# One step of an NF4 weight tile cut into two halves between the steps of the main work

## The reference, cut to what matters

```python
    def _dequant(codes, scales):
        w = NF4[codes]
        O, I = w.shape
        w = w.reshape(O, I // BLOCK, BLOCK) * scales[:, :, None]
        return w.reshape(O, I)
    def _lin_lora(x, W, A, B):
        base = jnp.einsum('bsh,oh->bso', x, W)
        lora = jnp.einsum('bsr,or->bso', jnp.einsum('bsh,rh->bsr', x, A), B)
        return base + lora
    q, k, v = (_lin_lora(x, _dequant(codes_attn[i], scales_attn[i]), ...) for i in range(3))
    attn = (q + k + v) / 3.0
    o = _lin_lora(attn, _dequant(codes_attn[3], scales_attn[3]), ...)
    x1 = x + o
    g = _lin_lora(x1, ...)          # 1792 features, gate
    u = _lin_lora(x1, ...)          # 1792 features, up
    h = jax.nn.silu(g) * u
    d = _lin_lora(h, ...)
    return x1 + d
x = x + _L0_attn_ref(_layernorm(x), ...)
x = x + _L0_ffn_ref(_layernorm(x), ...)
x = x + _L1_attn_ref(_layernorm(x), ...)
x = x + _L1_ffn_ref(_layernorm(x), ...)
```

## Time and profile before

| | |
|---|---|
| median of 3 runs | 804.11 us (802.1 to 804.88) |
| the profiled execution, its own time | 802.01 us |
| its span from first to last instruction | 800.7 us |
| TensorE busy | 718.0 us, 90% of the span |
| VectorE busy | 554.1 us, 69% |
| ScalarE busy | 448.2 us, 56% |
| GpSimd busy | 218.6 us, 27% |
| mean granted TensorE clock | 0.949 of 2.4 GHz |

### The profile page before, as it was taken

One profiled execution on the slowest core, in us unless ns is written; L12 is line 12 of the kernel. 1 busy time (PEld: TensorE's weight loads), 2 busy tenths in 40 slices (PEclk: granted clock), 3 DMA queues, 4 the chain that ended last, 5 costly groups with the idle time before them and its releaser, 6 DMA issues.

```text
span 800.7 us, 10753 instructions
## 1 busy us (share of the span) xinstructions
PE 718.0 (90%) x3832; PEld 535.9 (67%) x3832; DVE 554.1 (69%) x1065; ACT 448.2 (56%) x579; POOL 218.6 (27%) x208
## 2 busy tenths in 40 slices
PE   2898866999999998989988999988899999989998
PEld 1665422656677665667666777766677789967886
DVE  6979977563597767869798876667554434577883
ACT  3778787565877767877875722354432221244452
POOL 1023000004374653646577454211401000000000
PEclk9999966999999999989998999999999999979999
DMA  9636689867476677657765310201301011200001
GB/s 349 184 137 213 188 271 280 263 203 228 129 227 194 204 229 231 205 189 241 228 211 189 97 41 27 76 19 48 105 15 50 23 40 29 61 1 14 27 27 40
DMA packets 55541, 110.79 MB, mean 138 GB/s; under 512 B 9904, under 2 KB 20560, under 8 KB 55232
## 3 DMA queue, kind: packets, MB, share of 16 engines
q1 hardware_dynamic: 42912, 80.28, 31.4%
q10 hardware_dynamic: 8192, 15.73, 5.9%
q0 software_dynamic: 4384, 14.09, 5.9%
HBM read 92.19 MB, written 17.89 MB: 137 GB/s over the span
## 4 chain that ended last, share of the span: by engine, by line
PE 56%; DVE 19%; ACT 9%; issue 9%; DMA 4%; POOL 1%; ACTq 1%; SPq 1%; DVEq 0%; POOLq 0%
PE bank L1245 15%; PE bank L1247 14%; PE bank L1246 14%; ACT hot L1667 2%; PE bank L1359 2%; DVE x L2034 2%; DMA wide_buf<-in_down_flat 2%; ACT c L1627 2%; DVE bank L1949 2%; PE bank L1557 1%; DVE hot L1923 1%; PE bank L1372 1%; PE bank L1401 1%; DVE stats L1844 1%; ACT w_h L1675 1%
## 5 line engine op out<-in xcount | busy, mean ns | idle before, releaser
L1667 ACT ACTIVATE hot<-rep,levels 128x2048 f16<-128x2048 f16 x94 | 192.9, 2093 | 16.7 <-ACT c L1627 10.6
L1245 PE MATMUL bank<-zt_h,w_h 128*128 128x512 f32 (+1 forms) x232 | 94.8, 409 | 2.2 <-DVE zt_l L2022 2.0
L1247 PE MATMUL bank<-zt_h,w_l 128*128 128x512 f32 (+1 forms) x232 | 92.6, 399 | 0.0
L1246 PE MATMUL bank<-zt_l,w_h 128*128 128x512 f32 (+1 forms) x232 | 92.4, 398 | 0.0
L1245 PE MATMUL bank<-w_h,xq_h 128*128 128x512 f32 (+1 forms) x192 | 73.8, 384 | 2.2 <-ACT xq_l L1759 1.9
L1246 PE MATMUL bank<-w_l,xq_h 128*128 128x512 f32 (+1 forms) x192 | 71.6, 373 | 0.0
L1247 PE MATMUL bank<-w_h,xq_l 128*128 128x512 f32 (+1 forms) x192 | 71.5, 372 | 0.0
L1359 PE MATMUL bank<-hot,diag 128*32 128x512 f16 x856 | 64.7, 421 | 2.5 <-ACT hot L1667 2.5
L2178 POOL TENSOR_TENSOR q_a<-q_a,q_m 128x384 f32<-128x384 f32 (+3 forms) x34 | 35.7, 1051 | 85.1 <-DVE q_m L1808 85.0
L2240 POOL TENSOR_TENSOR at_l<-ztok,at_h 128x512 fp32r<-128x512 f32 x28 | 37.5, 1341 | 56.0 <-ACT at_h L1699 55.9
L1245 PEld LDWEIGHTS bank<-zt_h,w_h 128*128 128x128 f32 (+1 forms) x232 | 44.6, 192 | 12.0 <-DVE zt_l L2022 2.4
(11 more groups left out here) (221 smaller groups left out, 1703.1 us busy)
## 6 DMA issues: line engine op xcount, KB each, us to landing
rep<-codes SPq DMA_DIRECT2D x56, 512.0 KB, 4.7
codes<-c SPq DMA_DIRECT2D x28, 256.0 KB, 5.1
raw<-in_codes_gu_t ACTq DMA_DIRECT2D x14, 512.0 KB, 6.1
sc<-in_scales_gu_t SPq DMA_DIRECT2D x56, 128.0 KB, 3.2
raw<-in_codes_attn_t ACTq DMA_DIRECT2D x7, 512.0 KB, 3.8
raw<-in_codes_down_t ACTq DMA_DIRECT2D x7, 512.0 KB, 7.1
sc<-in_scales_down_t SPq DMA_DIRECT2D x28, 128.0 KB, 3.5
wide_buf<-in_gate_flat SPq DMA_DIRECT2D x5, 512.0 KB, 4.7
```

The lines of the kernel that those rows point to most:

```text
L1245: PE.matmul(psum, lh, rh, start=first, stop=False, **kw)
L1246: PE.matmul(psum, lh, rl, start=False, stop=False, **kw)
L1247: return PE.matmul(psum, ll, rh, start=False, stop=last, **kw)
L1667: S.activation(hots[plan.slot[hot_ring(t), (t, m)]][:], codes_in_place(t), ACT.Relu, bias=levels[:, at:at + 1], scale=levels[:, at + 1:at ...
```

## The change

The generator now yields twice per tile. The first half of step t holds the lookup of tile t, the LoRA product of tile t - 1, the parts of tile t - 2, the planes of tile t + 1. The second half holds the scaling of tile t itself and the transfer of scales. Rates are doubled, so that the same number of tiles goes by per main step. The two opening steps of the generator (its first loads; the planes of tile 0) aren't halved, so the tiles stand up to one step earlier in `stages`. `maxima` advances at half its rate while `until` runs before `attention`.

```diff
-EARLY_RATE = 0.7
-ATT_RATE = 0.5
-NF4_RATE = 0.43
+EARLY_RATE = 1.4
+ATT_RATE = 1.0
+NF4_RATE = 0.86
...
         if jobs[t // 2]["last"]:
             p.add("lora", t)
             p.note("made", t)
+            unsettled.append(t)
 
     def assemble(t):
...
-        if j["last"]:
-            unsettled.append(t)
...
             if t < tiles:
                 look(t)
             if t:
-                assemble(t - 1)
                 lora(t - 1)
             low_parts()
             if t + 1 < tiles:
                 hits(t + 1)
-            if t:
-                scales(t + 2)
             if t and u == 0:
                 if i > 1:
                     stacks(i - 1)
                 made[0] = i
+            yield
+            if t < tiles:
+                assemble(t)
+                scales(t + 3)
             yield
...
-    side_max = Side(greatest, MAX_RATE)
+    side_max = Side(greatest, MAX_RATE / 2)
     weave(stages(), Side(itertools.chain(int4_weights(), greatest), INT4_RATE), Side(ready_nf4, EARLY_RATE))
     until(n_attn - 1, side_max)
+    side_max.rate = MAX_RATE
```

## The result

The changed kernel takes 790.75 us, the median of 4 runs (787.44 to 791.87); the kernel before took 803.23 beside it (4 runs). The ratio is 0.984, 95% interval 0.981 to 0.987: faster by some 12.5 us, 1.6%, where 21 were forecast. The profiled execution took 790.65 us, span 789.3.

A forecast was written before the change was run, and what follows sets the result against it. TensorE was taken to set the pace from 200 to 480 us, waiting for late scalings and losing clock; VectorE and ScalarE from 60 to 137. Terms summed to -21.1 us, from 804.1 to 783 us, range 774 to 799.

The forecast's parts named there:

- rival A: All terms come as summed: 783 us, own range 774 to 791, chance 0.57.
- Rival B: The waits go but the clock doesn't come back: 792 us, range 789 to 799, chance 0.26.
- Waits of L1372: LoRA product waiting for its bank's scaling, 200 to 480 us: 16.8 us of waits, 4 left, so -12.8 us.
- The clock in that stretch: 200 to 480 us: of 11.2 us lost to slow clock, put down to these waits, 7.7 come back.
- Next in line: With TensorE faster in the stretch, planes and additions come late more often: +4 us, bounds 0 and +10.
- The start: Cast of token tile 1's high part slips behind the first plane: +3 us, bounds 0 and +6.8.
- Layer norms: 60 to 137 us: most of 4.1 us of waits for the sum behind the scaling goes: -2 us.
- one tile earlier: 100 to 137 us: ScalarE's queue, which TensorE waits for, holds one plane less: -2 us, bounds 0 and -4.
- Attention: Scaling of tile 20 moves ahead of what delayed it: 1.9 us of wait and 1.7 of clock, -3.6 us.
- D: Rival, down steps: the scaling pushes the additions, each costing 2.4 us; slower, 812 us at 12 tiles, chance 0.09.

The follow-up runs named there:

- kernel 12: The changed kernel measured once more, with nothing changed and a trace of its own: 788.86 us, ratio 0.982 to the kernel before.
- Kernel 10: The kernel before, with TensorE's waits of over 1 us for the bank filled by repeats of a lookup's first matmuls: 802.89 us, ratio 0.998.
- kernel 5: The kernel before, with scaling and load of next scales at the end of a still whole step from tile 23 on: 799.18 us, ratio 0.993.

## Why the prediction was right in kind and too large

The time lies in the range and in rival A's own range; 783 was 6 to 8 us too low. The time alone would not tell A from B: 790.75 lies in B's range too and nearer to its 792. What tells them apart is the clock. Two traces of the changed kernel give the terms (kernel 12 in second place).

- **Waits of L1372**, forecast -12.8: -16.1 and -16.6. Nearly nothing of them is left, where I had kept 4.
- **The clock in that stretch**, forecast -7.7: busy time for the same matmuls -7.5 and -7.1. Rival B, that the clock doesn't come back, fell: 1.00 instead of 0.96. Kernel 10 ties the slow slices to these places. The slow stretch at 340 us, for which the prediction had no wait in its rows, has one too, of 2.35 us up to 341.50.
- **Next in line**, forecast +4: +9.6 and +8.0 (all other waits of TensorE in the stretch, 5.6 us before, are 15.2 and 13.6). This is the term that was mis-sized most. The largest part is +5.9 and +4.2 for ScalarE's planes, and its cause was in no step of mine: I counted the moved `scales` as moved, but not that SP would stand in it with the spread of the codes behind. Kernel 6, with only that load put back, has 4.2 us of these waits instead of 8.4.
- **The start**, forecast +3, bounds 0 to +6.8: the first addition slipped by 5.5 us, the cast exactly as rows 9 had it, 18.84 to 25.63. By the last addition of the first product +3.9 and +3.0 were left, so this term was about right. The sign given for it was not: around 60 us the main work was up to 6.6 us behind, not 3 at most.
- **Layer norms** and **one tile earlier**, forecast -2 each: from the last addition of the first product to the merge it took 77.8 us before, 77.7 and 77.8 after, so 0 for both. These two terms are the step that failed. The waits for the sum behind the scaling did go, 4.1 to 0.3, and ScalarE's queue did hold one plane less. The third layer norm, from the last addition of the second product to the merge, became 4.1 and 3.8 us shorter. But the tile's work that left it now stands ahead of it, in the second product, where VectorE was already busy 32.2 of 34.6 us, and that stretch became 4.0 and 3.7 us longer. I had put this price at nothing. All eight traces with half steps have both (38.1 to 39.8 us and 39.0 to 41.2), all six with whole steps neither (34.1 to 34.7 and 42.6 to 44.7). That the moved tile is the cause is argued from the counts of instructions.
- **Attention**, forecast -3.6: 0 in the first trace, -4.8 in the second. The wait for the LoRA product went in both. What I had not seen is that the clock of this stretch is different from trace to trace, 0.90 and 0.97 here, by as much as the term: TensorE's busy time there is 53.9 us before, 54.3 and 50.8 after, its waits are 5.7, 5.3 and 4.0.
- **D**, the scaling pushes the additions: waits for x went from 1.7 to 4.2 and 3.5 us, where I had set "under 4", and far from the 10 of D. With whole steps (kernel 5) they are 9.6: additions do come late behind what stands ahead of them, and the halves hold it down.

By these terms the two traces give 3.8 + 0 - 14.1 = -10.3 and 3.0 - 4.8 - 15.8 = -17.6 up to the last `gu_mul`, and the spans fell by 11.4 and 17.6. The medians, 12.5 and 15.4 us below those beside them, lie between.

## What to carry to other kernels

A wait at one instruction is a matter of how far ahead its producer stands in the queues; but moving the producer without dividing the step handed most of the wait on to the work that then stood behind it (a gain of 4.8 us in the stretch, against 17.1 with the step divided). When a step is moved, follow its transfers too: a load that waits for the moved work holds every later transfer of the same issuing engine, and putting one load back was worth 6 to 9 us, about half of what the change itself brought. Work that is moved out of one stretch arrives in another: look at how busy the engines are there as well. Cut a stretch by marks of the work, not by fixed times: busy time and waits of the same matmuls then add up to its length, and the clock can be read apart from the waits. And take a second trace before a few microseconds in one stretch are explained.

## What the runs showed of the hardware

The granted clock over 10 us fell to about 0.84 beside waits of TensorE of 1.1 to 2.4 us, in the middle of dense work. With work put in at seven such places of the NF4 stretch (kernel 10) one slow slice was left of ten. In the NF4 stretches of all 14 traces the clock fell to the lower level 33 times, each time beside or shortly behind a wait of 1 us or more: for the scaling, for an addition to x, or for planes. The reverse doesn't hold: about half of such waits had no fall near them. The two traces of the changed kernel show it at the same lookup. In the first all slices from 200 to 520 us are at 1.00, in kernel 12 those from 410 and 420 us are at 0.94 and 0.89:

```profile
425.78 0.40 PE L1360 MATMUL bank<-hot,diag 128*32 128x512 f16 x4 [1.58 <-ACT hot L1668]
```

```profile
417.44 0.40 PE L1360 MATMUL bank<-hot,diag 128*32 128x512 f16 x4 [1.59 <-ACT hot L1668]
```

No fall came without a wait, and the wait alone doesn't decide it. What does stays open.
